# Three sums and products of a gated transformer kernel moved off the vector engine, its steps cut into pieces, and the hand-written order rewritten

## What is computed

```python
# layer 0: performer attention; then 16-head attention feeding 8 linear experts, top 2
out = att + sum_e comb[:, e] * (y @ W[e]) + comb @ b
# layer 1: 8 heads of 64, softmax over the 64 largest scores of 256; gated experts, top 2
h = silu(y @ gate_w) * (y @ up_w);  expert = h @ down_w
# layer 2: 16-head attention; GELU experts 128 -> 512 -> 128, top 2 of 8
# layer 3: 16 heads of 8, softmax over the 32 largest scores; mixture attention with 16 experts
w = softmax over the chosen experts
q, k, v = (sum_e w_e * (y @ P_e) for P in (q_proj, k_proj, v_proj))
out = sum_e (w_e * softmax(q k^T / sqrt(128)) v) @ o_proj[e]
```

## Time and profile before

| | |
|---|---|
| median of 3 runs | 2431.43 us (2431.41 to 2431.61) |
| the profiled execution | 2433.76 us, its span 2432.0 us |
| PE busy | 2103.5 us, 86% of the span |
| DVE busy | 2045.2 us, 84% |
| ACT busy | 1353.8 us, 56% |
| POOL busy | 912.7 us, 38% |
| mean granted TensorE clock | 0.942 |

### The profile page before, as it was taken

One profiled execution on the slowest core, in us unless ns is written; L12 is line 12 of the kernel. 1 busy time (PEld: TensorE's weight loads), 2 busy tenths in 40 slices (PEclk: granted clock), 3 DMA queues, 4 the chain that ended last, 5 costly groups with the idle time before them and its releaser, 6 DMA issues. The chain is left out here.

```text
span 2432.0 us, 41472 instructions
## 1 busy us (share of the span) xinstructions
PE 2103.5 (86%) x12569; PEld 1629.8 (67%) x12569; DVE 2045.2 (84%) x8036; ACT 1353.8 (56%) x3311; POOL 912.7 (38%) x1422
## 2 busy tenths in 40 slices
PE   5878798989988899988988899898999899887776
PEld 3556567656876678666876679665886568666455
DVE  1399897989989798998989899898989899896971
ACT  2435356566646556566556557475555666476431
POOL 4142213634264233634155233633246332433422
PEclk9888899999999999999999999999999999898687
DMA  4000001000100001000100001000010001001000
GB/s 178 1 7 1 27 14 46 1 2 26 53 10 1 27 5 57 1 1 27 49 14 1 27 1 55 8 1 27 23 40 1 1 27 53 29 5 49 1 3 3
DMA packets 29502, 55.02 MB, mean 23 GB/s; under 512 B 2914, under 2 KB 10082, under 8 KB 28642
## 3 DMA queue, kind: packets, MB, share of 16 engines
q1 hardware_dynamic: 29282, 52.37, 6.6%
HBM read 51.31 MB, written 1.05 MB: 22 GB/s over the span
## 5 line engine op out<-in xcount | busy, mean ns | idle before, releaser
L219 DVE MATCH_REPLACE8 top_work<-top_eight,top_work 128x256 f32<-128x256 f32 x1664 | 667.1, 408 | 0.0
L221 DVE MAX8 top_eight<-top_work 128x8 f32<-128x256 f32 x1664 | 617.7, 412 | 0.3
L255 POOL TENSOR_TENSOR top_p<-top_p,top_rest 128x512 f32<-128x512 f32 x192 | 245.4, 1278 | 180.4 <-ACT top_rest L248 179.3
L738 PE MATMUL bank<-workP 128*128 128x256 f32 x1024 | 278.7, 396 | 29.0 <-ACT att_pP L868 23.3
L868 ACT ACTIVATE att_pP<-bank,att_nmaxP 128x256 f32<-128x256 f32 x512 | 214.9, 478 | 80.7 <-DVE att_nmaxP L917 80.0
L738 PEld LDWEIGHTS bank<-workP 128*128 128x128 f32 x1024 | 181.0, 194 | 78.2 <-issue 52.5
L221 DVE MAX8 top_lead<-bank 128x8 f32<-128x256 f32 x384 | 144.8, 418 | 61.8 <-PE bank L550 39.3
L890 POOL TENSOR_SCALAR workP<-workP,const 128x256 f32<-128x256 f32 x256 | 121.3, 479 | 198.8 <-PE bank L738 142.4
L248 ACT ACTIVATE top_rest<-top_work,top_nmax 128x256 f32<-128x256 f32 x384 | 173.7, 506 | 34.0 <-DVE top_work L219 33.7
L917 DVE TENSOR_REDUCE att_nmaxP<-bank 128x2 f32<-128x512 f32 x256 | 171.7, 683 | 23.4 <-PE bank L738 22.0
L227 POOL TENSOR_SCALAR top_nmax<-top_lead 128x2 f32<-128x2 f32 x192 | 36.8, 192 | 407.6 <-DVE top_lead L221 407.0
(11 more groups left out here) (331 smaller groups left out, 4538.5 us busy)
## 6 DMA issues: line engine op xcount, KB each, us to landing
gelu_w<-in_pack3w SPq DMA_DIRECT2D x72, 256.0 KB, 3.0
top_qk<-in_pack3w SPq DMA_DIRECT2D x72, 256.0 KB, 2.8
pack<-in_pack SPq DMA_DIRECT2D x1, 4352.0 KB, 19.9
pack<-in_pack SPq DMA_DIRECT2D x1, 2266.0 KB, 10.0
pack<-in_pack SPq DMA_DIRECT2D x1, 1028.0 KB, 7.5
mix_wb<-in_ctx SPq DMA_DIRECT2D x1, 1024.0 KB, 5.0
x_in<-in_x SPq DMA_DIRECT2D x8, 128.0 KB, 2.1
ctx_tok<-in_ctx SPq DMA_DIRECT2D x8, 128.0 KB, 2.3
```

Of the source, the lines that this page charges most:

```text
L219: ins = nc.vector.match_replace(self.work[:, u % 2, j, :], eight, src, GONE)
L221: ins = nc.vector.max(eight, src)
L255: self.k.nc.gpsimd.tensor_tensor(v, v, self.rest[:, :, :], ALU.subtract).then_inc(self.p_ready, 1)
L738: mm = self.k.nc.tensor.matmul(self.banks[u % 2][:, j * T:(j + 1) * T], self.q1[:, u % self.RING, j * P:(j + 1) * P], self.kT, start=True, ...
```

## The change

Three pieces of arithmetic leave the vector engine:

- Linear experts: ACT copies each expert's 128 columns out of PSUM scaled by its weight (16 activations a block), and GpSimd adds the eight terms of a tile as a tree of three additions (4x128, 2x128 and 128 columns), then adds the attention's output (128 columns).
- Gated experts in one bank: ACT copies half of b out of PSUM (one more activation a unit), the vector engine keeps u = (th+1)*a, and GpSimd multiplies the two. ACT's tanh now also waits for GpSimd's previous product.
- Mixed attention: all eight `attended` products are GpSimd's, except in the last block, where `Chunk4` runs alone and keeps the old turns.

`link` and `group` are replaced by `mark` and `ready`, and a vector step may be cut: `yield` ends a piece, and the wait is issued only at the start of the next piece. `cuts(s)` says how many cuts a step has. A letter of the order now stands for a piece; the other engines issue their part of a step with its last piece. Pairs of instructions for the two tiles, which waited one by one, are marked together with a single wait behind both. All six orders are new strings. `TopSelect.select` is cut between its two MAX8 and its two MATCH_REPLACE8. In `GatedExperts` the router's step comes behind the unit's products instead of ahead of them.

```diff
 class Chain:
-    def link(self, eng, ins):
-        self.n += 1
-        ins.then_inc(self.sem, 1)
-        eng.wait_ge(self.sem, self.n)
+    def mark(self, *instructions):
+        self.n += len(instructions)
+        for ins in instructions:
+            ins.then_inc(self.sem, 1)
+
+    def ready(self, eng):
+        eng.wait_ge(self.sem, self.n)
...
 class Router:
-        for j in range(NT):
-            link(v.max(self.m8[:, j, :], self.pr[:, j, 0:E8]))
-        link(v.memset(self.m8[:, :, 2:8], SENT))
-        for j in range(NT):
-            link(v.match_replace(self.wk[:, j, :], self.m8[:, j, :], self.pr[:, j, :], GONE))
+        chain.mark(*(v.max(self.m8[:, j, :], self.pr[:, j, 0:E8]) for j in range(NT)))
+        yield
+        chain.ready(dve)
+        chain.mark(v.memset(self.m8[:, :, 2:8], SENT))
+        yield
+        chain.ready(dve)
+        chain.mark(*(v.match_replace(self.wk[:, j, :], self.m8[:, j, :], self.pr[:, j, :], GONE) for j in range(NT)))
...
-        dve.wait_ge(self.comb_ready, 1)
...
 class LinearExperts(Units):
     def act(self, act, s):
-        pass
+        u = self.at(s, 0, 0)
+        if u >= 0:
+            j, part = divmod(u, self.parts)
...
+            act.wait_ge(self.y_ps, u + 1)
+            for i in range(self.PART):
+                e = self.PART * part + i
+                ins = self.k.nc.scalar.activation(self.terms[:, j, e, :], self.banks[2 + part][:, i * D:(i + 1) * D], ACT.Copy,
+                                                  scale=self.rt.comb[:, j, e:e + 1])
+            ins.then_inc(self.taken, 1)
     def pool(self, pool, s):
-        pass
+        u = self.at(s, 0, 0)
+        if u >= 0 and u % self.parts == self.parts - 1:
+            j = u // self.parts
+            pool.wait_ge(self.taken, u + 1)
+            half = E8 // 2
+            while half:
+                upper, lower = self.terms[:, j, half:2 * half, :], self.terms[:, j, 0:half, :]
+                self.k.nc.gpsimd.tensor_tensor(lower, lower, upper, ALU.add).then_inc(self.added, 1)
...
+            self.k.nc.gpsimd.tensor_tensor(acc, acc, self.att.o[:, j, :], ALU.add).then_inc(self.added, 1)
...
 class GatedInOneBank(Units):
             act.wait_ge(self.h_ps, u + 1)
+            nc.scalar.activation(self.hT[:, u % 2, :], self.bank[:, T:2 * T], ACT.Copy, scale=0.5).then_inc(self.half_ready, 1)
+            if u >= 1:
+                act.wait_ge(self.hT_ready, u)
             nc.scalar.activation(self.th, self.bank[:, 0:T], ACT.Tanh, scale=0.5).then_inc(self.th_ready, 1)
...
+            pool.wait_ge(self.half_ready, u + 1)
+            pool.wait_ge(self.u_ready, u + 1)
+            hT = self.hT[:, u % 2, :]
+            self.k.nc.gpsimd.tensor_tensor(hT, hT, self.th, ALU.mult).then_inc(self.hT_ready, 1)
...
-            dve.wait_ge(self.u_ready, u + 1)
-            nc.vector.scalar_tensor_tensor(out=self.hT[:, u % 2, :], in0=self.th, scalar=0.5, in1=b[:, T:2 * T],
-                                           op0=ALU.mult, op1=ALU.mult).then_inc(self.hT_ready, 1)
...
 class MixedAttention(Units):
-        if 0 <= i < self.PAIRS and i % 2 == 1:
+        if 0 <= i < self.PAIRS and (i % 2 == 1 or not self.alone):
             pool.wait_ge(self.o_copied, 1)
             self.attended(nc.gpsimd, i).then_inc(self.zo2_ready, 1)
...
+def vector_part(dve, stage, s, part, last, under_way):
+
+    if part == 0:
+        under_way[stage] = stage.dve(dve, s) or iter(())
+    if last:
+        assert sum(1 for _ in under_way[stage]) == 0
+    else:
+        next(under_way[stage])
```

361 lines of the change are left out of this document (244 added, 117 removed).

## The result

The changed kernel takes 2397.04 us (median of 4 runs, 2396.57 to 2397.45), against 2431.52 for the kernel before in the same comparison: ratio 0.986, 95% interval 0.984 to 0.987. It is faster by 34.5 us. I forecast 2331 and a range of 2285 to 2392. The direction was right, the size was not: a third of the forecast 100 us arrived, and the time lies above the range.

The account below looks back on a forecast made before the run. Vector engine bounds HEADS; it and TensorE are near their limit in WIDE; lane waits set WIDE_2 and LAST. Of 130 us (72.6+42.6+14.9), 101.5 arrive, less 1.4: 100 off 2433.8 gives 2333.7, runs 2331; range 2285 to 2392.

Parts of the forecast that it names:

- a microsecond less of its work is nearly a microsecond less of block: HEADS blocks: the vector engine, busy 130.1 of 143.8 us, hardly stands still; 10.5 of 12.1 us a block arrive.
- The orders themselves I cost at nothing, between -20 and +20.: All six new order strings: no effect on time by themselves, bounds -20 to +20 us.
- Gated: Gated experts: 0.45 us of vector work goes per unit, ten times in six blocks: 27 us.
- a unit has a tenth of a block, some 13 us, to itself: Gated units: the chain grows by 0.7 us, but each unit has some 13 us of room.
- Linear: Linear experts: sixteen multiply-adds leave each sequence, 6.4 us, 7 of 8 sequences beside another lane: 45 us.
- Attended: Mixed attention: 28 products leave the vector engine at 0.92 us each: 25.6 us, bounds 19 and 49.
- Links: Vector waits: 119 grouped and 149 filled cuts at 0.12 us: 32 us, bounds nothing to twice that.
- rival 4: A link costs nothing once other work fills its place: about 25 us less arrives, 2356; chance 0.07.
- What was said to show it: Changed kernel's trace: vector engine busy about 1947 us, ACT 1425, GpSimd 1040; HEADS 133, WIDE 131; MAX8 411 to 413 ns.
- Rival 1: TensorE and hand-overs hold the blocks: WIDE gives 1 us, HEADS 6, the rest 6; 48 us, 2383; chance 0.17.
- Rival 3: GpSimd's queue delays the top lane's `negative_max` in HEADS: at 2 us a head, slower, 2495; chance 0.07.
- Rival 5: Shared port: GpSimd's new work holds the vector engine, 121 us come back, 9 left: 2424; chance 0.03.

Follow-up runs that it names:

- no_moves: Changed kernel with linear, gated and attended products back on the vector engine, new orders and pieces kept: 2468.09 us, 1.015 to the kernel before.
- linear kept: Changed kernel with only the linear experts' sum back on the vector engine: 2439.14 us, 1.0023 to the kernel before.
- gated kept: Changed kernel with only the gated product back on the vector engine: 2381.06 us, 0.979 to the kernel before.
- old orders: Changed kernel, all moves and pieces, under the six orders of the kernel before, letters repeated per piece: 2536.56 us, 1.043 to the kernel before.
- pair of spare copies: Kernel with the gated product on the vector engine (2381.06) plus one unread ACT copy a unit: behind tanh 2384.87 us, ahead of it 2399.05.
- no_attended: Changed kernel with attended products shared between vector engine and GpSimd as before: 2439.01 us, 1.0022 to the kernel before.
- keep_copy: Changed kernel with the gated product on the vector engine from SBUF, ACT's half copy kept: 2410.34 us, 0.991 to the kernel before.

## Why the prediction was wrong

**The first step that failed: "a microsecond less of its work is nearly a microsecond less of block".** I read the earlier trace rows, few waits of the vector engine in HEADS, as a proof that the vector engine sets the block's length. It was a picture of an order whose letters fitted that work. HEADS blocks in these runs, vector engine's busy time against length: 130.0 in 147.7 (no moves), 130.1 in 143.8 (before), 127.8 in 149.5 (linear kept), 124.4 in 142.0 and 124.5 in 140.1 (gated kept), 122.1 in 143.4 (the change), 122.2 in 158.0 (old orders). Across orders and hand-overs the length does not follow the busy time. Within one order it can: the linear move takes 5.7 us of busy time out of a HEADS block and 6.2 of its length. Of the 63 us forecast for HEADS 2.2 came, and the runs show how: new orders and pieces add 28 us to the six blocks (859.9 to 888.1), the linear move, with the attended one that has no instruction there, takes 43 away (to 845.4), and the gated move adds 12 (to 857.7).

**"The orders themselves I cost at nothing, between -20 and +20."** It left its bounds on both sides (a minus is faster): +37 without the moves, pieces included, +47 against the same pieces in the old letters (2468.09 - 2420.93), -140 with the moves. This is the largest error of the sum. I treated the six strings as a neutral carrier of the other edits; they decide whether an edit arrives. Nor could the term be had from the trace of before: it shows where the old letters fit, not where the new ones do.

**Gated: +27 became -16.** The arithmetic is right: 60 instructions left, 24.9 us of work with 415 ns each stayed. The failed step is "a unit has a tenth of a block, some 13 us, to itself", and with it "I cost both at nothing" for ACT. The 0.38 us copy stands between TensorE's product and tanh, and the vector engine is already there. The pair of spare copies shows that the place matters: the same activation costs 18 us ahead of tanh and about 4 behind it. In HEADS the loss goes along with a longer time at TensorE's lower clock, a path that the forecast did not have at all.

**Linear: 45 forecast, 42 measured.** Right in size, and the only move whose work lay in lane P's own chain. It is 6.2 of 6.4 us in each HEADS block.

**Attended: 25.6 forecast, of which 3.7 a WIDE block; 42 measured, 6.0 a WIDE block.** The sign is right, the term too small, and that is partly luck: the work that left is less than I said, 20.6 us instead of 28, and the gain is larger. The 28 instructions take 753 ns each in no_attended, and in the kernel before they took 925; my mean of 996 had in it the four of the last block, 1.49 us each, that stay. What I did not count is the standing ahead of these instructions, 35.0 us under the new letters against 4.4.

**Links: 32 forecast.** The grouped part, 119 waits or 14 us, measured 11 by itself, so rival 4, a link that costs nothing, falls for the part that could be measured alone; in WIDE blocks of equal clock the price is about half of the 0.12 us from the earlier trace rows. By the page "VectorE: DVE Perf Modes" of the Trainium skill, section "The DRAIN you can't avoid", a semaphore costs nothing extra, and the part would have been nothing; the trace and this run go against that. The same section also says that a next operation that is not held starts earlier than the emptied pipe, and with that the 0.08 us between independent neighbours agrees. The filled cuts were mis-sized: together with the grouped waits they give 72 us under the new orders, more than any price of a link read here.

**What was said to show it.** ACT 1425: 1426.1. GpSimd 1040: 1030.6. MAX8 at 411 to 413 ns: 411. A WIDE block at 131: 133.3. A HEADS block at 133: 143.4. The vector engine at 1947: 1948.9, but not by the sum 2045-45-25-28. The page of no_moves has it busy 2024.3, so orders and pieces took 21 where I had said that a link is no busy time (instructions without a wait between them overlap in the record), and the moves took 75: 45.5, 12.8 and 17.3 for linear, gated and attended, by the pages of the three kernels without one. Gated and attended were 23 too high: the former mostly because other instructions grew by 10.6, the latter because the 28 instructions that left were shorter, as said above, and overlap with their neighbours.

**The rivals.** Rival 1 (2383) came nearest in time, for the wrong reason: it expected WIDE to give 1 us a block and HEADS 6; WIDE gave 3.5 and HEADS 0.4. Rival 3 named GpSimd's queue; the gated move did turn into a loss, but taking GpSimd's part away and keeping the copy (keep_copy) gained nothing, and a copy alone costs as much. The top lane's wait for `negative_max` is 2.6 us of the block, on ACT. Rival 5 was dismissed by MAX8 alone. MAX8 is not held, but L482, L1336 and L315 are, for 10.6 us with the gated move, an eleventh of what the rival priced. The Trainium skill, "SBUF — State Buffer", section "Who interferes with whom", says that a vector instruction in a two-port mode contends with GpSimd too, names the tensor-scalar form (L482 and L315) among those that can enter one, and says that whoever issues first then blocks the other for the whole instruction. L482 agrees: it begins second and ends with GpSimd's addition. I had used that rule for MAX8 alone.

**What stays open.** Why the new letters are 47 us dearer than the old ones when nothing is moved. In HEADS, 30 of these 47, the named waits of the vector engine are 15.6 against 8.0 us a block; putting the start back made it slower. How much of each loss is TensorE's clock: over the whole kernel the mean granted clock is 0.928 with the old orders and the moves, 0.933 with no moves, 0.943 in the change and 0.954 with the gated product kept. And whether an order written for the version without the gated move would gain more than the 50 us of 2381.06; none was tried.

## What to carry to other kernels

In a kernel whose queues run in an order written by hand, few waits on an engine can mean that the order fits the engine's work, and do not prove that a new order will keep it so: the order and the edits must be costed and measured together, and an edit alone under the old order can lose 116 us where both gain 34. Cost an instruction added to a less busy engine by what stands directly behind it in that queue and who waits for that; here a copy of 0.42 us ahead of the awaited result cost 18 us in 60 uses, and about 4 behind it. Compare blocks of equal granted clock before a small difference is given to an edit: here it went along with half of that loss. When an edit bundles several moves, take out one at a time: here one of three was a loss, and without it the kernel gains 50 us instead of 34.

## What the runs showed of the hardware

A small vector instruction can be held for the whole of a GpSimd instruction that began just ahead of it: L482, 32 columns, 1.25 us beside an addition of 1.26, and 0.18 otherwise; a product of 256 columns from two SBUF operands 425 ns alone and up to 1446 beside GpSimd, and with one operand in PSUM 420 to 423 either way. MAX8 and MATCH_REPLACE8 kept their 411 and 407 ns. In this kernel, which repeats its blocks, the meeting of L482 comes back in each of the six.

Across a block's end TensorE is busy 0.89 of 3.60 us, and the granted clock falls to the lower of its two levels, 1.2 and 2.4 GHz. It is back at full 8.5 us into the next block, so that the block's first tenth has a mean of 0.70. The columns are those of the tables above, in the changed kernel:

```profile
664.70:668.30 3.60, 0.89 (x4) 0.31 (x3) 0.17 (x1) 1.27 (x4) 0.00 (x0) 0.75 0.00 0
668.30:671.90 3.60, 3.58 (x12) 2.80 (x12) 0.09 (x1) 0.60 (x1) 0.94 (x2) 0.50 0.37 109
...
679.00:682.60 3.60, 3.60 (x20) 3.14 (x19) 1.01 (x5) 1.61 (x4) 0.09 (x1) 1.00 0.00 0
```

The same group of instructions shows both levels, in the timeline of TensorE (start and duration):

```profile
669.20 1.92 PE L586 MATMUL bank<-top_qk 128*128 128x256 f32 x4
...
680.59 1.03 PE L586 MATMUL bank<-top_qk 128*128 128x256 f32 x4
```

TensorE is busy 13.60 of the first 14.30 us, so the lower level is paid where it is full. The idle gap alone does not fix how much that is: with the gated product kept, TensorE idles 2.25 us at the end of the block before 672.1 and 2.34 before 946.9, and the blocks that follow have a granted clock of 0.97 and 0.99 and last 142.0 and 140.1 us. The kernel with the longest HEADS blocks also has the lowest clock in them (0.93 at 158.0 us).
